# Four stacked graph layers on one core: the layers' small weight loads are issued in the preparation stage

## What is computed

```python
x = _layernorm(x + layer_k(x, weights_k, adj), axis=-1)
```

## Time and profile before

| what | before |
|---|---|
| median of 3 executions | 2121.07 us (2120.79 to 2121.31) |
| the profiled execution's own time | 2120.09 us |
| its span, first to last instruction | 2118.3 us |
| busy: PE, PEld | 1941.9 us (92%), 1202.4 us (57%) |
| busy: DVE, ACT, POOL | 1622.3 us (77%), 1253.9 us (59%), 581.1 us (27%) |
| mean granted TensorE clock | 0.96 of full speed |
| DMA | 42.17 MB, 7.5% of the 16 engines' time on the queue of SP |
| stage starts (SP's first issue) | first 22.86, second 272.73, third 484.75, fourth 734.16 us |

### The profile page before, as it was taken

One profiled execution on the slowest core, in us unless ns is written; L12 is line 12 of the kernel. 1 busy time (PEld: TensorE's weight loads), 2 busy tenths in 40 slices (PEclk: granted clock), 3 DMA queues, 4 the chain that ended last, 5 costly groups with the idle time before them and its releaser, 6 DMA issues.

```text
span 2118.3 us, 51578 instructions
## 1 busy us (share of the span) xinstructions
PE 1941.9 (92%) x22228; PEld 1202.4 (57%) x22228; DVE 1622.3 (77%) x1909; ACT 1253.9 (59%) x2298; POOL 581.1 (27%) x454
## 2 busy tenths in 40 slices
PE   6999759986999489999999999999999999999993
PEld 5888647765888344545455455455455454554542
DVE  3999738875999567787887887887878878878763
ACT  3677656652777545665665655656656656656552
POOL 0233348871333200021221221211212212212214
PEclk8999969997999779999999999999999999999996
DMA  6000000000000000101101101101001011011010
GB/s 160 3 4 3 3 1 1 1 1 2 4 3 3 6 1 21 23 11 37 27 12 37 26 12 37 26 12 37 22 17 27 11 37 27 11 37 26 12 37 21
DMA packets 45227, 42.17 MB, mean 20 GB/s; under 512 B 32072, under 2 KB 35720, under 8 KB 45000
## 3 DMA queue, kind: packets, MB, share of 16 engines
q1 hardware_dynamic: 45000, 38.88, 7.5%
HBM read 25.76 MB, written 4.72 MB: 14 GB/s over the span
## 4 chain that ended last, share of the span: by engine, by line
PE 58%; DVE 4%; POOL 1%; issue 1%; ACT 0%; DMA 0%; SPq 0%; POOLq 0%; ACTq 0%; DVEq 0%
PE fourth_ps_out L1373 21%; PE fourth_ps_scores L1325 7%; PE fourth_ps_out L1387 6%; PE fourth_ps_scores L1328 5%; PE fourth_ps_scores L1331 5%; PE fourth_ps_prep L1291 3%; DVE fourth_weights L1031 3%; PE fourth_ps_scores L1349 2%; PE fourth_ps_prep L1300 1%; PE fourth_ps_scores L1358 1%; PE fourth_ps_scores L1352 1%; PE fourth_ps_scores L1355 1%; PE fourth_ps_prep L1284 1%; PE fourth_ps_prep L1262 1%; DVE fourth_cat L1010 1%
## 5 line engine op out<-in xcount | busy, mean ns | idle before, releaser
L1031 DVE TENSOR_TENSOR fourth_weights<-fourth_weights,keep_mask 128x1024 f32<-128x1024 f32 x512 | 663.0, 1335 | 127.6 <-ACT fourth_weights L1180 125.6
L1180 ACT ACTIVATE fourth_weights<-fourth_ps_scores 128x1024 f32<-128x1024 f32 x512 | 497.4, 1024 | 363.6 <-PE fourth_ps_scores L1331 343.0
L1373 PE MATMUL fourth_ps_out<-fourth_weights,fourth_x_stage 128*64 128x512 f32 x2048 | 498.0, 605 | 4.6 <-DVE fourth_weights L1031 4.6
L1373 PEld LDWEIGHTS fourth_ps_out<-fourth_weights,fourth_x_stage 128*64 128x64 f32 x2048 | 124.3, 136 | 249.5 <-issue 202.2
L1325 PE MATMUL fourth_ps_scores<-fourth_g_high,fourth_x_high 64*128 64x512 f32 x1024 | 230.5, 446 | 2.4 <-DVE fourth_g_low L998 2.4
L1325 PEld LDWEIGHTS fourth_ps_scores<-fourth_g_high,fourth_x_high 64*128 64x128 f32 x1024 | 96.3, 184 | 201.1 <-issue 101.4
L1328 PE MATMUL fourth_ps_scores<-fourth_g_high,fourth_x_low 64*128 64x512 f32 x1024 | 203.2, 393 | 0.0
L1331 PE MATMUL fourth_ps_scores<-fourth_g_low,fourth_x_high 64*128 64x512 f32 x1024 | 201.6, 390 | 0.0
L1187 ACT ACTIVATE fourth_weights<-fourth_ps_scores 128x1024 f32<-128x1024 f32 x128 | 124.9, 1025 | 113.8 <-PE fourth_ps_scores L1358 113.8
L1038 DVE TENSOR_TENSOR fourth_weights<-fourth_weights,keep_mask 128x1024 f32<-128x1024 f32 x128 | 153.2, 1237 | 43.4 <-ACT fourth_weights L1187 43.4
L899 POOL TENSOR_TENSOR fourth_biased<-fourth_mixed,fourth_rows_in 128x512 f32<-128x512 f32 x16 | 33.2, 2078 | 473.2 <-DVE fourth_mixed L1046 473.2
(11 more groups left out here) (265 smaller groups left out, 3044.8 us busy)
## 6 DMA issues: line engine op xcount, KB each, us to landing
fourth_recip_wide<-recip_out SPq DMA_DIRECT2D x64, 256.0 KB, 3.9
setup_adj<-in_adj SPq DMA_DIRECT2D x8, 512.0 KB, 6.5
fourth_h_high<-fourth_h_high SPq DMA_DIRECT2D x32, 128.0 KB, 4.1
fourth_h_low<-fourth_h_low SPq DMA_DIRECT2D x32, 128.0 KB, 3.7
out<-keep_x SPq DMA_DIRECT2D x16, 256.0 KB, 2.6
dens_out<-fourth_mixture SPq DMA_DIRECT2D x64, 4.0 KB
keep_x<-in_x SPq DMA_DIRECT2D x1, 512.0 KB, 11.0
fourth_dens<-dens_out SPq DMA_DIRECT2D x32, 8.0 KB, 1.6
```

The source lines that it names most:

```text
L1031: dve.tensor_tensor(buf, buf, keep.mask[:, st.t, cols(half)].bitcast(F32).unsqueeze(1) .to_broadcast([P, 2, HALF]), ALU.mult).then_inc(wei ...
L1180: act.activation(weights[st.slot + half][:, :], ps_scores[half][:, :], ACT.Exp)\
L1373: last = pe.matmul(ps_out[rows(g), cols(half)], x_stage[st.s][:, st.t, g, :], weights[st.slot + half][:, cols(g)], start=(st.t == 0), stop ...
```

## The change

All 22 small loads leave the layers' blocks and stand in `setup`'s block behind the loads of `adj` and of the first two batches of `x`, in the order of the layers. Their targets and the semaphores they count on now belong to `Keep`, one semaphore for each additive layer, one for the feature layer, one for the dot layer. The memset of `bias_rows` moves from the fourth layer's POOL to `setup`'s POOL, between the memset of `row_used` and the wait before `row_used`'s ones and the identity, and POOL waits for it there. The waits of the layers' compute engines stay where they were, now on the kept semaphores. The feature layer's SP has nothing left to do; L360's load stays in the first layer.

```diff
 def setup(nc, ins, keep):
...
                 sp.dma_start(keep.x[:, 0:2, :, :], x_rows(ins)[:, 0:2, :, :]).then_inc(keep.first_x_loaded, 16)
+                for layer, (w_name, a_name) in enumerate((("L0_gnn_W", "L0_gnn_a"), ("L2_gnn_W", "L2_gnn_a"))):
+                    for half in range(2):
+                        sp.dma_start(keep.w[layer][half * DIM:(half + 1) * DIM, :], ins[w_name])\
+                          .then_inc(keep.additive_loaded[layer], 16)
+                    for k in range(2):
+                        sp.dma_start(keep.a_cols[layer][:, k:k + 1], ins[a_name][k * DIM:(k + 1) * DIM, :])\
+                          .then_inc(keep.additive_loaded[layer], 16)
+                sp.dma_start(keep.scalars[:, 0:1], ins["L1_gnn_w0"].to_broadcast([P, 1])).then_inc(keep.feature_loaded, 16)
+                sp.dma_start(keep.scalars[:, 1:2], ins["L1_gnn_b0"].unsqueeze(0).to_broadcast([P, 1]))\
+                  .then_inc(keep.feature_loaded, 16)
+                sp.dma_start(keep.factor_row[:, :], ins["L1_gnn_wa"].unsqueeze(0).to_broadcast([P, DIM]))\
+                  .then_inc(keep.feature_loaded, 16)
+                sp.dma_start(keep.bias_col[:, :], ins["L1_gnn_ba"].unsqueeze(1)).then_inc(keep.feature_loaded, 16)
+                for g in range(2):
+                    sp.dma_start(keep.wh_in[:, g, :], ins["L3_gnn_Wh"][2 * g:2 * g + 2, :, :]
+                                 .rearrange("h d c -> (h d) c")).then_inc(keep.dot_loaded, 16)
+                sp.dma_start(keep.wo_in[:, :], ins["L3_gnn_Wo"]).then_inc(keep.dot_loaded, 16)
+                for k, name in enumerate(("L3_gnn_bo", "L3_gnn_gamma", "L3_gnn_beta")):
+                    sp.dma_start(keep.rows_in[:, k, :], ins[name].unsqueeze(0).to_broadcast([P, DIM]))\
+                      .then_inc(keep.dot_loaded, 16)
+                sp.wait_ge(keep.bias_cleared, 1)
+                for h in range(HEADS):
+                    at = (h % 2) * DIM
+                    sp.dma_start(keep.bias_rows[at:at + 1, h, :], ins["L3_gnn_bh"][h:h + 1, :])\
+                      .then_inc(keep.dot_loaded, 16)
...
                 pool.memset(row_used[:, :], 0.0).then_inc(consts, 1)
+                pool.memset(keep.bias_rows[:, :, :], 0.0).then_inc(keep.bias_cleared, 1)
+                pool.wait_ge(keep.bias_cleared, 1)
                 pool.wait_ge(consts, 6)
...
-def additive_layer(nc, stage, keep, w_in, a_in, x_in=None):
+def additive_layer(nc, stage, keep, layer, x_in=None):
...
-        w = sb("w", [P, DIM])
+        w, a_cols, loaded = keep.w[layer], keep.a_cols[layer], keep.additive_loaded[layer]
...
             def _(sp):
-                for half in range(2):
-                    sp.dma_start(w[half * DIM:(half + 1) * DIM, :], w_in).then_inc(loaded, 16)
-                for k in range(2):
-                    sp.dma_start(a_cols[:, k:k + 1], a_in[k * DIM:(k + 1) * DIM, :]).then_inc(loaded, 16)
                 if x_in is not None:
                     sp.dma_start(keep.x[:, 2:BATCH, :, :], x_in[:, 2:BATCH, :, :]).then_inc(keep.x_loaded, 16)
...
 def dot_layer(nc, stage, keep, ins, out):
...
-                pool.memset(bias_rows[:, :, :], 0.0).then_inc(bias_cleared, 1)
```

More of the change, by code:

```diff
@@ L291, in additive_layer @@
         PAIRS = TILES // 2
-        w = sb("w", [P, DIM])
+        w, a_cols, loaded = keep.w[layer], keep.a_cols[layer], keep.additive_loaded[layer]
         w_turned = sb("w_turned", [DIM, 2, DIM])
-        a_cols = sb("a_cols", [DIM, 2])
         a_wide = sb("a_wide", [DIM, P + 1])
@@ L325, in additive_layer @@
         empty_tile = sem("empty_tile")
-        loaded, w_full, w_ready, prod_full, prod_ready = (
-            sem(n) for n in ("loaded", "w_full", "w_ready", "prod_full", "prod_ready"))
+        w_full, w_ready, prod_full, prod_ready = (
+            sem(n) for n in ("w_full", "w_ready", "prod_full", "prod_ready"))
         x_full, x_ready, tile_top_ready, s1_full, hidden_full, hidden_ready = (
@@ L695, in dot_layer @@
         BUILT = TILES + 2 * HEADS + 2 * HEADS
-        wh_in = sb("wh_in", [P, 2, DIM])
+        wh_in, wo_in, rows_in, bias_rows = keep.wh_in, keep.wo_in, keep.rows_in, keep.bias_rows
+        loaded = keep.dot_loaded
         wh_twice = sb("wh_twice", [P, 2, 2, DIM])
-        bias_rows = sb("bias_rows", [P, HEADS, DIM])
         form_high = sb("form_high", [P, PAIRS, P], F32R)
@@ L702, in dot_layer @@
         post = sb("post", [P, PAIRS, P])
-        wo_in = sb("wo_in", [DIM, CAT])
         wo_twice = sb("wo_twice", [DIM, HEADS, 2, DIM])
         wo_stack = sb("wo_stack", [P, PAIRS, DIM])
-        rows_in = sb("rows_in", [P, 3, DIM])
         minus_sum = sb("minus_sum", [P, P], F32R)
@@ L743, in dot_layer @@
         ps_prep = mem.psum("ps_prep")
-        loaded, bias_cleared, set_up, twice_ready, prods_full, form_ready, built = (
-            sem(n) for n in ("loaded", "bias_cleared", "set_up", "twice_ready", "prods_full", "form_ready", "built"))
+        set_up, twice_ready, prods_full, form_ready, built = (
+            sem(n) for n in ("set_up", "twice_ready", "prods_full", "form_ready", "built"))
         staged, x_full, x_high_ready, x_low_ready = (sem(n) for n in ("staged", "x_full", "x_high_ready", "x_low_ready"))
@@ L816, in _ @@
             def _(sp):
[L817 to L826, removed]
                 out_v = out.rearrange("b (t p) d -> p b t d", p=P)
@@ L1487, in feature_layer @@
         HALF_TILES = TILES // HALVES
-        scalars = sb("scalars", [P, 3])
-        factor_row = sb("factor_row", [P, DIM])
-        bias_col = sb("bias_col", [DIM, 1])
+        scalars, factor_row, bias_col, loaded = keep.scalars, keep.factor_row, keep.bias_col, keep.feature_loaded
         scaled = sb("scaled", [P, TILES, DIM])
@@ L1517, in feature_layer @@
         ps_back = [mem.psum(f"ps_back{k}", (P, HALF)) for k in range(HALVES)]
-        loaded, scale_ready = sem("loaded"), sem("scale_ready")
+        scale_ready = sem("scale_ready")
         scaled_ready, positive_ready, decayed_ready, soft_ready = (
@@ L1559, in feature_layer @@
         with nc.Block() as block:
[L1561 to L1568, removed]
             @block.gpsimd
@@ L1890, in __init__ @@
         self.minus_half = mem.sbuf("minus_half", [P, TILES])
+        self.w = [mem.sbuf(f"w{k}", [P, DIM]) for k in range(2)]
+        self.a_cols = [mem.sbuf(f"a_cols{k}", [DIM, 2]) for k in range(2)]
+        self.scalars = mem.sbuf("scalars", [P, 3])
+        self.factor_row = mem.sbuf("factor_row", [P, DIM])
+        self.bias_col = mem.sbuf("bias_col", [DIM, 1])
+        self.wh_in = mem.sbuf("wh_in", [P, 2, DIM])
+        self.wo_in = mem.sbuf("wo_in", [DIM, HEADS * DIM])
+        self.rows_in = mem.sbuf("rows_in", [P, 3, DIM])
+        self.bias_rows = mem.sbuf("bias_rows", [P, HEADS, DIM])
+        self.additive_loaded = [mem.semaphore(f"additive_loaded{k}") for k in range(2)]
+        self.feature_loaded = mem.semaphore("feature_loaded")
+        self.dot_loaded = mem.semaphore("dot_loaded")
+        self.bias_cleared = mem.semaphore("bias_cleared")
 def build(nc, ins, out):
@@ L1896, in build @@
         setup(nc, ins, keep)
-        additive_layer(nc, "first", keep, ins["L0_gnn_W"], ins["L0_gnn_a"], x_rows(ins))
+        additive_layer(nc, "first", keep, 0, x_rows(ins))
         feature_layer(nc, "second", keep, ins)
-        additive_layer(nc, "third", keep, ins["L2_gnn_W"], ins["L2_gnn_a"])
+        additive_layer(nc, "third", keep, 1)
         dot_layer(nc, "fourth", keep, ins, out)
```

## The result

The changed kernel takes 2102.19 us (median of 4 executions, 2102.03 to 2102.90) against 2120.93 us of the kernel before in the same comparison: a ratio of 0.9914, 95% interval 0.9897 to 0.9931, 18.7 us less. The forecast was 2101.3 us, a gain of 19.8. The profiled execution took 2102.32 us with a span of 2100.5 us, 17.8 less than the 2118.3 of before.

A forecast was written before the change was run, and what follows sets the result against it. PE-busy loops fill the layers, untouched; each layer's start waits for small loads, 20.3 us in all. Terms 3.8 + 4.5 + 3.7 + 6.8 + 1.0 = 19.8 us off 2121.07 give 2101.3 us, range 2096.5 to 2106.5.

The forecast's parts named there:

- first layer's start: First layer: PE's first matmul 4.2 us earlier, less 0.4 for a DVE copy held beside POOL's memsets; 3.8 us (3.5 to 4.2).
- third layer's start: Third layer, same code as the first: 4.1 us of waiting gone, less 0.4; 3.7 us gained (3.4 to 4.1).
- second layer's start: Second layer: ACT's first pass starts right behind its table load, at 274.1 instead of 278.59; 4.5 us gained (3.2 to 4.5).
- fourth layer's start: Fourth layer: DVE starts 6.2 us earlier, PE's gain depends on whether DVE precedes POOL's copies; 6.8 us (5.9 to 7.6).
- the clock: the rest of the four layers: All layers: PE's clock rises earlier against the work; 1.0 us gained, extremes -3.4 to +3.4.
- preparation stage: In setup: SP's 22 added issues finish by 18.3, inside a stage ending at 22.09; 0 us (0 to 0.5 lost).
- DVE slipping through ahead of POOL's copies: Fourth layer: DVE's subtractions and copy of `Wo` precede POOL's copies, so PE starts up to 1.4 us earlier still, 7.6 in all.
- Rival 3: In setup: SP's queue holds each added issue until a landing, 2.1 us each, stage grows 29 us; 2130 us; chance 0.04.
- SP's issues running past 22: In setup: sign that the forecast is wrong; SP's last issue was expected by 18.3.
- the microsecond that the prediction had named as a sign of being wrong: Any layer: the forecast is wrong if the length from its first matmul changes by more than a microsecond.
- Rival 2: Layer starts: the clock stays up, PE could begin the first layer at full clock; 22.7 us gained, 2098.4 us; chance 0.14.
- The load of 14 batches: First layer: the load of `x` lands at 43.2, PE needs it at 44.5; stays hidden with 1.3 us left.

## Why the prediction was right, and where it was off

The forecast of 2101.3 us was 0.9 off the median, and its range held. The mechanism was right at all four layer starts and wrong in the preparation stage, and part of the nearness is luck: by the two profiles the gain was 17.8 us where 19.8 was forecast, made up of 2.5 lost in the preparation stage and 0.6 less from the clock against 1.05 more in the fourth layer. The medians come nearer mostly because the profiled execution of before lay 1.0 us under its median. The parts, each from the stage starts and the instructions that the last column names:

| term | forecast | measured | how |
|---|---|---|---|
| first layer's start | 3.8 | 3.82 | PE's transposition at 6.33 us into the layer, now 2.51 |
| third layer's start | 3.7 | 3.71 | 6.22, now 2.51 |
| second layer's start | 4.5 | 4.54 | ACT's pass at 5.84, now 1.30 |
| fourth layer's start | 6.8 | 7.85 | PE at 9.02, now 1.17 |
| the clock: the rest of the four layers | 1.0 | 0.37 | +0.10, +0.97, -1.05, +0.35 |
| preparation stage | 0 | -2.49 | first layer starts at 25.35, not 22.86 |
| sum | 19.8 | 17.8 | spans: 2118.3 - 2100.5 |

**First and third layer.** Right to 0.1 us, and for the reason given: no wait but for the barrier, and a DVE copy that stands still beside POOL's memsets. The copy was `a_wide` at 1.03 us, and taking the memsets out of its way returned the 0.4 at PE's second product. The size, 0.4, was chosen between 0 and 0.7. The prediction spoke of standing still for one POOL instruction; here the copy, at 25.46 to 26.49, outlasted the memset that it met (0.52 us from 25.35) and ended only with the second of that length.

**Second layer.** Right, with the reserve that the old wait itself was 1.0 us shorter in another execution. The row of the table load was the next wait; with it moved the pass came another 0.36 us earlier. The Trainium skill (ScalarE: Activation LUTs, What ACT_TABLE_LOAD costs) adds about 1380 ns of drain to the load. Here the load takes 1.28 us and the next pass starts 0.02 us behind its end, so in this place, behind a barrier with ACT idle, that part is not there, and the measurement decides.

**Fourth layer.** The mechanism was right and the size off by 1.0: of the two cases in the prediction, DVE slipping through ahead of POOL's copies (7.6) is the one that happened, and the middle value was a compromise between cases. Even that case was set too low: the 6.2 of the loads and the 1.67 that the prediction had read from its own rows make 7.9, as measured, and it had counted 1.4 of the 1.67. The Trainium skill (SBUF — State Buffer, SBUF: two separate sides) says that the loser of the shared port waits for the winner's whole instruction. The 1100 and 1050 ns beside POOL's copies of 1.02 to 1.03 us, and the 250 ns without them, agree. What decided here was the order at the start: POOL had memsets until 726.1 and its copies came second.

**The preparation stage.** This is the step that failed: "so the issues lie beside other work with 3.8 us to spare", with a term of 0 (0 to 0.5 lost). It cost 2.49 us. The price of each issue came from small loads issued into a queue that was nearly empty. Behind the load of `x` the first of them took 8.25 us. Rival 3 had named the place and the threshold (0.77 us per issue), but it bore its price on every issue; the hold falls once, and 8.2 + 21 x 0.5 us went 2 us beyond the slack (0.88 us per issue on average). The eight fast issues of `adj`, cited against it, said nothing on the short pieces of `x`. The prediction's own sign for this, SP's issues running past 22, came. A hint stood in the trace of before: in the second layer one small load took 1.74 us to issue, where in the kernel with POOL's copies held back that one took 0.43 and the next one 1.58. So issues are also held by about a microsecond with nothing large ahead; why is open.

**The clock.** The rest of the four layers gave 0.37 instead of 1.0, within the bounds of 3.4 on either side: the second layer gained what the third lost, the third by more than the microsecond that the prediction had named as a sign of being wrong. Nothing in the profile of before told the sign per layer; a term of 0 with bounds would have been as well founded. Rival 2 didn't come about: in the kernel after PE begins the first layer at the low level, its first matmul taking 0.28 us. In the eight profiles in which SP is done early this first matmul runs at the high level (0.21 us), but the clock falls between 23.4 and 26.0 us in all of them; in four the product behind it is still at the high level too (0.49 us instead of 0.79), and in two of these the transposition comes 0.3 us sooner. No more than that is seen of rival 2.

**The load of 14 batches** stayed hidden, as said: issued at 25.40, landed 19.5 us later at 44.9, needed at 46.91.

## What to carry to other kernels

A load issued and awaited at the head of a stage behind a barrier costs its full latency (here 4.1 to 6.2 us each time), and moving the issue into an earlier stage returns it down to the next wait, which can be read off the same timeline: memsets, a table load, a DVE copy that takes 1.03 us instead of 0.21 beside memsets. Before adding issues to a queue, look at what stands ahead of them: put small loads ahead of a transfer with many short pieces, not behind it, and count the queue's time against the barrier that it must reach. In differences of about a microsecond, compare the moment of the clock's rise before crediting or blaming an edit.

## What the runs showed of the hardware that was not expected

An issue on SP's queue is held behind an earlier transfer of many short pieces until that one is under way: 8.25 us behind 512 KB in pieces of 256 bytes that themselves stood behind `adj`, and 17.43 us behind 14 batches (which the trace lists as packets of 1024 bytes, though the access pattern has the same pieces). Nine transfers of 512 KB in 4 KB rows ahead don't hold it at all (issues stay at 0.6 us). And with the moment at which TensorE's clock rose against the work, the second layer's rest went between 205.0 and 206.4 us and the third's between 242.9 and 244.4, with the same code.
